# Four GNN layers on one core: Pool's pacing writes removed, a 2048-byte descriptor ring, and fewer gather columns on TensorE

## The reference

```python
h = jnp.maximum(_layernorm(x), 0.0)
# layer 0: rows of h by source, times an edge pattern, mean by destination
msg = rel[src] * pattern;  h_N = segment_sum(msg, dst) / jnp.maximum(deg, 1.0)[:, None]
# layer 1: attention over edges
scores = jnp.sum(Q[receiver] * K[sender], axis=1) * scale
alpha = jnp.exp(scores - segment_max(scores, receiver)[receiver])
out = segment_sum(alpha / Z * V[sender], receiver)
# layer 2: agg = segment_sum(X[src_idx], dst_idx); return agg @ W
# layer 3: six couplings of node_irreps[edge_index[0]] with edge harmonics, summed by target
```

## Time and profile before

| | |
|---|---|
| median of 3 runs | 16013.85 us (15978.6 to 16015.91) |
| span of the profiled execution, first to last instruction | 14816.7 us |
| median less that span | 1197.2 us |
| TensorE busy | 12890.3 us, 87% of the span |
| Pool busy | 12431.7 us, 84% |
| VectorE busy | 9612.6 us, 65% |
| ScalarE busy | 3874.6 us, 26% |
| mean granted TensorE clock | 0.948 of full speed |

### The profile page before, as it was taken

The page is one execution under the profiler, slowest core; times in us unless marked ns, Lnnn a source line. Parts: engine busy times, 40 slices in busy tenths (PEclk is TensorE's granted clock), DMA queues, the critical chain, the costliest instruction groups (busy, mean ns, idle before and its releaser), DMA issues.

```text
span 14816.7 us, 226154 instructions
## 1 busy us (share of the span) xinstructions
PE 12890.3 (87%) x57644; PEld 10677.8 (72%) x57644; DVE 9612.6 (65%) x13223; ACT 3874.6 (26%) x4265; POOL 12431.7 (84%) x18594
## 2 busy tenths in 40 slices
PE   7999999992699999999689999999769999999996
PEld 6888888881577777777578888888756666767764
DVE  7666666664577777777666666666656665666665
ACT  2222222220233333333222222222211111111111
POOL 6888888887888888888778888888888888888884
PEclk9999999995899999999889999999989999999998
DMA  5444444442344444444345555545433333333332
GB/s 174 148 148 157 157 155 151 149 151 46 101 123 122 124 124 123 122 123 124 90 119 130 129 130 128 131 127 131 110 76 87 86 90 83 90 86 87 87 86 56
DMA packets 1340717, 1727.48 MB, mean 117 GB/s; under 512 B 501932, under 2 KB 1145566, under 8 KB 1339646
## 3 DMA queue, kind: packets, MB, share of 16 engines
q10 hardware_dynamic: 705956, 1154.87, 24.6%
q1 hardware_dynamic: 327194, 407.86, 9.6%
q0 software_dynamic: 306880, 158.96, 7.6%
HBM read 1140.23 MB, written 580.36 MB: 116 GB/s over the span
## 4 chain that ended last, share of the span: by engine, by line
POOL 41%; issue 32%; PE 20%; DVE 5%; POOLq 1%; DMA 0%; DVEq 0%; ACT 0%; ACTq 0%; SPq 0%
POOL rows L492 22%; POOL pace L497 16%; PE psum L690 12%; PE psum L773 7%; POOL outs L509 2%; PE psum L764 2%; DVE work L1340 1%; DVE work L1315 1%; POOLq L496 1%; POOL q_edges L471 1%; POOL work L501 1%; DVE tile_rows L924 0%; DVE work L1323 0%; DVE rows L931 0%; DVE outs L1347 0%
## 5 line engine op out<-in xcount | busy, mean ns | idle before, releaser
L690 PE MATMUL psum<-h_parts,one_hot 128*128 128x448 f32 x49406 | 10813.2, 377 | 482.0 <-ACT one_hot L539 262.4
L690 PEld LDWEIGHTS psum<-h_parts,one_hot 128*128 128x128 f32 x49406 | 9428.8, 192 | 1500.6 <-ACT one_hot L539 313.0
L492 POOL DMA_INDIRECT rows<-h_table,idx x9000 | 8662.9, 963 | 1966.9 <-POOL pace L497 1537.1
L546 ACT ACTIVATE one_hot<-keys 128x896 fp32r<-128x896 bf16 x2533 | 2359.9, 950 | 6435.5 <-PE psum L690 4314.0
L497 POOL MEMSET pace<- 128x288 f32 x9000 | 3213.9, 357 | 18.1 <-issue 13.2
L924 DVE TENSOR_TENSOR tile_rows<-psum,h_mask 128x448 f32<-128x448 f32 x2722 | 1686.2, 619 | 1252.3 <-PE psum L690 991.3
L931 DVE TENSOR_REDUCE rows<-tile_rows 128x32 f32<-128x448 f32 x2722 | 1677.0, 616 | 58.9
L773 PE MATMUL psum<-work,bd_t 128*128 128x512 f32 (+1 forms) x3500 | 1359.2, 514 | 240.1 <-DVE work L1323 141.3
L1323 DVE TENSOR_TENSOR work<-psum,work 128x800 f32<-128x800 f32 x875 | 862.7, 988 | 920.9 <-PE psum L764 864.2
L773 PEld LDWEIGHTS psum<-work,bd_t 128*128 128x128 f32 x3500 | 654.9, 193 | 764.4 <-issue 443.4
L912 DVE TENSOR_REDUCE rows<-psum 128x32 f32<-128x448 f32 x807 | 503.1, 623 | 792.0 <-PE psum L690 741.7
(11 more groups left out here) (202 smaller groups left out, 6198.1 us busy)
## 6 DMA issues: line engine op xcount, KB each, us to landing
keys<-hots ACTq DMA_DIRECT2D x2542, 224.0 KB
keep_in<-keep_flat SPq DMA_DIRECT2D x2000, 100.0 KB
sums<-outs ACTq DMA_DIRECT2D x375, 400.0 KB
rows<-h_table,idx POOLq DMA_INDIRECT x9000
hots<-bit_hot ACTq DMA_DIRECT2D x506, 224.0 KB
hots<-work ACTq DMA_DIRECT2D x506, 224.0 KB
attn<-outs ACTq DMA_DIRECT2D x125, 800.0 KB
edge_in<-pattern_c SPq DMA_DIRECT2D x125, 400.0 KB
```

The costliest lines, as they stand in the source:

```text
L492: nc.gpsimd.indirect_dma_start(out=rows[:, r, j * D:(j + 1) * D], out_offset=None, in_=h_table[:, :], in_offset=bass.IndirectOffsetOnAxis( ...
L546: nc.scalar.activation(one_hots[i % LOOK[l]][:, :, :], loaded_hots[i % BIT_BUFS[l]], ACT.Copy).then_inc(one_hot_cast, 1)
L690: last = nc.tensor.matmul(banks[TILE_BANKS[l][b]][:, 0:H0 * D], one_hots[hot][:, h1, :], h_parts[:, part, h1 * H0 * D:(h1 + 1) * H0 * D], ...
```

## The change

PE_COLS hands fewer columns to TensorE (32, 24, 32 and 20 of the 125 of a turn), and so more to Pool (93, 101, 93 and 105). The memsets, their tile and their two semaphores are gone. A chunk's gathers are split in two halves, each with a semaphore of its own, and VectorE waits for both. The memory that holds Pool's DMA descriptors is set to 2048 bytes per partition in place of the default, 16384.

```diff
-PE_COLS = ((8, 8, 8, 8, 8), (7, 7, 6, 6, 6), (8, 8, 8, 8, 8), (6, 6, 5, 5, 6))
-PACE = 288
+PE_COLS = ((7, 7, 6, 6, 6), (5, 5, 5, 5, 4), (7, 7, 6, 6, 6), (4, 4, 4, 4, 4))
+RING_BYTES = 2048
...
-        pace = sb("pace", [P, PACE])
...
-        rows_gathered = [sems(f"rows_gathered{a}_") for a in range(2)]
+        rows_gathered = [[sems(f"rows_gathered{a}_{side}_") for side in range(2)] for a in range(2)]
...
+        def half_of(l, r):
+
+            by_pool = J - PE_COLS[l][r]
+            return range(0, by_pool // 2), range(by_pool // 2, by_pool)
...
-            pool.sem_inc(pause_ended, START)
...
-                        for j in range(J - PE_COLS[l][r]):
-                            nc.gpsimd.indirect_dma_start(
-                                out=rows[:, r, j * D:(j + 1) * D], out_offset=None, in_=h_table[:, :],
-                                in_offset=bass.IndirectOffsetOnAxis(ap=idx[:, r, j:j + 1], axis=0)).then_inc(rows_gathered[l % 2][r], 16)
-                            pool.wait_ge(pause_ended, pauses(l, t, r, j))
-                            pool.sem_inc(pause_begun, 1)
-                            nc.gpsimd.memset(pace[:, :], 0.0).then_inc(pause_ended, 1)
+                        for side, columns in enumerate(half_of(l, r)):
+                            for j in columns:
+                                nc.gpsimd.indirect_dma_start(
+                                    out=rows[:, r, j * D:(j + 1) * D], out_offset=None, in_=h_table[:, :],
+                                    in_offset=bass.IndirectOffsetOnAxis(ap=idx[:, r, j:j + 1], axis=0))\
+                                    .then_inc(rows_gathered[l % 2][side][r], 16)
...
-                v.wait_ge(rows_gathered[l % 2][r], gathers(l, t, r))
+                for side in range(2):
+                    v.wait_ge(rows_gathered[l % 2][side][r], gathers(l, t, r, side))
...
-    nc = bacc.Bacc("TRN2", target_bir_lowering=False, num_devices=1)
+    nc = bacc.Bacc("TRN2", target_bir_lowering=False, num_devices=1, dynamic_dma_scratch_size=RING_BYTES)
```

More of the change, by code:

```diff
@@ L263, in gnn_kernel @@
         x_ready, x_stored = sem("x_ready"), sem("x_stored")
-        pause_begun, pause_ended = sem("pause_begun"), sem("pause_ended")
         block = ctx.enter_context(nc.Block())
@@ L1160, in turn_in @@
                 r1, more = r % RING, r // RING
-                v.wait_ge(rows_gathered[1][r1], gathers(1, t, r1, more))
+                for side in range(2):
+                    v.wait_ge(rows_gathered[1][side][r1], gathers(1, t, r1, side, more))
                 v.wait_ge(picked, tile_no(tile_base, 1, t, first_tile(1, r + 1)))
@@ L1312, in next_rows @@
                 r1, more = (r + 1) % RING, (r + 1) // RING
-                v.wait_ge(rows_gathered[1][r1], gathers(3, t, r1, more))
+                for side in range(2):
+                    v.wait_ge(rows_gathered[1][side][r1], gathers(3, t, r1, side, more))
                 v.wait_ge(picked, tile_no(tile_base, 3, t, first_tile(3, r + 2)))
@@ L1348, in turn_messages @@
                 v.wait_ge(outs_ready[r], use(3, t))
-            v.wait_ge(rows_gathered[1][0], gathers(3, 0, 0))
+            for side in range(2):
+                v.wait_ge(rows_gathered[1][side][0], gathers(3, 0, 0, side))
             v.wait_ge(picked, tile_no(tile_base, 3, 0, first_tile(3, 1)))
```

9 lines of the change are left out of this document (3 added, 6 removed).

## The result

The changed kernel takes **20316.72 us** (median of 4 runs, 20305.24 to 20327.51). Beside it the kernel before takes 15996.23 us: ratio 1.2699 (95% interval 1.2678 to 1.272), 27% slower. Forecast was 14890 us, with a range of 14550 to 15700.

The account below looks back on a forecast made before the run. Pool was taken to bound layers 0 to 2, TensorE-VectorE alternation layer 3; afterwards layer 1 its own chain. By layer -243 - 190 - 243 - 451 = -1127 us; 16013.85 - 1127 = 14887, rounded to 14890 us, range 14550 to 15700.

Parts of the forecast that it names:

- What bounds the kernel now: Before the change: Pool bounds layers 0 to 2; in layer 3 the alternation of TensorE and VectorE, 153.3 us a turn.
- Part 1: Pool's loops: without memsets a gather costs 1.25 us instead of 1.47, plus each layer's remainder and 1.0 us a boundary.
- Part 3: Fewer TensorE tiles at about 3.0 us each: layers 0 and 2 stay Pool's, layer 1 gains 190 us, layer 3 451.
- The last line of the sum: Whole run: the runs' median lies 1197.2 us above the profiled span of 14816.7; kept, so 16013.85 - 1127 = 14887.
- Part 4: Two semaphores a chunk and the 2048-byte ring: taken as 0 us, bounds 0 and 1450; 14 gathers estimated to fit.
- C: Rival: the small ring makes Pool wait for a landing each half chunk, pitch 1.40 us; 16220 us, chance 0.08.
- D: Rival: in heavy DMA traffic a bare gather takes 1.47 us anyway; +919 us, 16930 us, chance 0.05.
- the boundary: Pool at each turn's end: 2.0 us more than the usual step before; 1.0 taken for after, bounds 0 and 2.0.
- The 4.8 us: Layer 0, per turn: gathers lengthened while VectorE works, kept in the sum; under the skill's rule 120 us less.
- Layer 1: Becomes bound by its own chain at 132.5 us a turn, above Pool's 128.7; -190 us.
- Layer 3: Turn falls from 153.3 us to 134 taken, chain some 129 to 136, Pool needing 133.3; -451 us.
- Pool near 90%: Sign that the forecast is right: Pool's busy share on the profile page of the changed kernel near 90%.

Follow-up runs that it names:

- e4: The kernel before with only the wait and the memset between gathers removed: 21391.7 us, 1.33 of before.
- e1: The changed kernel with the default ring in place of 2048 bytes: 20346.57 us, 1.265 of before.
- e2: The changed kernel with the wait and the 288-column memset put back behind every gather: 16182.75 us, 1.0093 of before.
- e5: The kernel before, unchanged, run again for a profile: 15279.38 us, 0.9998 of before.
- e15: The changed kernel unchanged, timed a third time, beside a before of 14816.69 us: 13478.12 us, 0.9097 of before.
- e6: The kernel before, its columns and pause kept, with the 2048-byte ring and two semaphores a chunk: 15219.73 us, 0.9967 of before.
- e3: The kernel before with the ring of 2048 bytes alone, one semaphore a chunk: 15666.41 us, 0.974 of before.
- 216 columns: Kernel before with 2048-byte ring, two semaphores a chunk, memset of 216 columns: 14302.93 us, 0.9655 of before.
- 144 columns: Kernel before with 2048-byte ring, two semaphores a chunk, memset of 144 columns: 13994.19 us (0.9451 of before), in another set 20217.51 us (1.3229).
- 288 columns: Full-length memset behind every gather, 2048-byte ring, two semaphores a chunk: 0.9967 of before with the old columns, 1.0093 with the change's.
- e9: The changed kernel with every loop gather fetching rows for 64 of the 128 partitions only: 13218.06 us, 0.8922 of before.
- e14: Kernel before with 2048-byte ring, two semaphores a chunk, 144-column memset, timed again beside a before of 15283.9 us: 20217.51 us, 1.3229.
- e8: The changed kernel with the wait and the 288-column memset behind every fourth gather only: 19820.92 us, 1.297 of before.

## Why the prediction was wrong

**"What bounds the kernel now" and Part 1 failed at one sentence.** I cost the removal of the memsets by Pool's own time and named nothing that they did for others. In a disturbed set the pause of 0.52 us between gathers keeps TensorE near its usual speed; without it TensorE starves and VectorE, ScalarE and Pool wait for it (e4, e1: +33% and +27%; e2 puts the pause back: 1.009). Pool's own prices were right in the disturbed runs too: a gather 950 ns, start to start 1.25 us in all layers. What failed is that TensorE's speed was taken as given: Part 3 took a tile at 3.0 us, with its signal at once, and so TensorE was "not the bound". Instead it stood still 1748 times without waiting for anything, and the picks of its tiles started 7210 us late in sum.

**The last line of the sum failed with it.** I put 1197.2 us "around the span" and carried them over as a constant. The runs' own spans show otherwise: 15275.2 of 15279 us in e5, 20325.7 of 20327.5 in the changed kernel. So the 1197 us lay inside the runs' spans. In e5 the 458 us above the profile shown go with lone matmuls and late picks; for the runs of 16014 us the same cause is likely, but no trace shows it. A median 8% above the span of the profiled execution was the one sign on the page, and I used it as an addend.

**My rivals named no such mechanism.** C and D had Pool slower and Pool as the bound; in the measured trace Pool is idle for half of the span. The small ring, C's cause, costs nothing with two semaphores: Part 4's zero held (e15 has no step above 3 us in layers 0, 2 and 3, e6 none of e3's waits, and e1 takes the time of the change). The semaphores are what buys it: with one, each chunk pays 2.24 us (e3).

**In the undisturbed set the sum can be checked.** From 14816.7 to 13479.7 are 1337 us; I had 1127.
- Pitch: 1.25 forecast, 1.249 measured, and no step above 3 us at the turns of layers 0, 2 and 3: the boundary costs nothing where I took 1.0.
- Layer 0: 117.3 us a turn against 122.1. The 4.8 us that I kept for gathers lengthened beside VectorE were mostly gone (93 x 1.249 = 116.2).
- Layer 1: 127.6 against 132.5. Seventeen turns take 126 us, paced by Pool, the last seven 129 to 133, near the chain that I had priced; the first ones run ahead into the free buffers.
- Layer 2: 116.9 against 118.3. Layer 3: 131.2 against 133.3 of Pool and 134 taken; it is Pool's, not the chain's.
- Between layers I had no change. From a layer's last gather to the next one's first the times grew from 403, 211 and 156 us to 441, 299 and 165, 134 us in all. Without this the sum would be off by more.
- One sign could not have come: "Pool near 90%". At 0.95 us in 1.25 it is 76% at most; the page has 73%.

So the mechanism of the forecast, Pool as the bound at 1.25 us a gather, was right for one condition and mis-sized by 210 us; layer 3, and seventeen of layer 1's 25 turns, were wrongly given to their chains. It was not the condition in which the change was timed.

**A rule weighed.** The Trainium skill, "SBUF — State Buffer", section "Who interferes with whom", infers that a two-input operation on VectorE holds up no descriptor generation. I kept 4.8 us against it by the row of 1.34 us. The reading of before was right: its gathers in layer 0 last 0.999 us in the mean where layer 1 has 0.951, which makes 4.1 us a turn. In the changed kernel long ones are still there (1.11 us at 2015.52), yet they add up to 1.1 us a turn (e15). So the rule came nearer to the sum than my term. But the rule doesn't explain it: with the pauses put back beside the same work of VectorE (e2) it is 3.9 us a turn again.

**What stays open.** What disturbs, and what TensorE and Pool share. That it lies outside the kernel is shown (one program, 13994 and 20217 us; before itself at several levels); its source is not. It isn't the chip alone: the sets fell on chips 0 (16043), 2 (15274 and 14813), 13 (15284), 14 (14817) and 6 (14819). It goes with the missing records of semaphore updates in every set; whether the recording itself disturbs, or suffers from the same thing, no run tells. Fetching of instructions has little to show for itself: the queues for it move the same 54 packets in both traces of the change,

```profile
q14 instruction: 38, 0.31, 0.0%
q8 instruction: 16, 0.26, 0.0%
```

while VectorE and ScalarE never stand still without a wait. Matmuls that wait for nothing and still stand, and signals that come late, both belong to TensorE, but the trace doesn't say whether a matmul really ends later than its record has it. Lumped pauses, half the transfers and 216 columns were never run in a disturbed set.

**No version that ran in both conditions is faster than before in both.** Undisturbed: the change 0.910, 144 columns 0.945. Disturbed: these lose 27% or more, while 288 columns stay within 1% of before with either set of columns (0.997, 1.009), and e3 with its accidental waits is at 0.974. 216 columns (0.966, undisturbed) is the candidate left untried.

## What to carry to other kernels

A filler instruction that nothing reads may be there for its neighbours: before taking out a pause on one engine, ask what the other engines do in it, and time the result more than once, at different times. When the profiled execution and the runs differ by more than a launch can explain, don't carry the difference as a constant; get a profile of a typical run first. And put the unchanged kernel, and the changed one, beside every set of experiments: without that, 144 columns would have passed for a cure that it isn't, and e9 and 216 columns for cures that nobody had tested. Last, when several engines stand still at once, ask for each whether its next instruction waits for a signal and whose: here one was held up and the others followed.

## What the runs showed of the hardware

- Pool's indirect gathers 1.25 us apart can starve TensorE: 1748 idle stretches of over 0.5 us without a wait, and signals to VectorE that come a median of 8.0 us late. In disturbed sets the edge lies between a start-to-start of 1.35 us (1.32 of before, e14) and 1.47 us (0.997, e6), with the same columns, ring and semaphores; in undisturbed ones 1.25 us is harmless (e15).
- More pause hardly helps up to 1.35 us: 1.25, 1.255, 1.305 (the mean of e8) and 1.35 us apart give 20088, 20794, 19821 and 19441 us with the change's columns (the second and third beside a before of 15274, the others beside 15284). How the time falls between 1.35 and 1.47 us wasn't measured.
- Starved TensorE advances in steps of about 0.70 us: lone matmuls start 1.41, 2.13, 1.39 and 2.83 us after one another from 2027.40 on, and 1681 of the trace's 1790 lone ones start within 0.1 us of a multiple of 0.70 us behind the matmul before.
- With a ring of 2048 bytes and one semaphore a chunk, Pool waits ahead of the fifteenth gather of each chunk, 2.24 us in the mean (e3); with two semaphores it doesn't (e6).
- The granted clock falls with the starving, from 0.89 to 0.97 by layer undisturbed to 0.73 to 0.80, and the mean matmul of line 683 grows from 387 to 397 ns. TensorE's busy time grows by 1028 us of the 6846 that the span grows, so most of the loss is idle time, which the lower clock doesn't explain.
